# Values as the moving operand, heads divided and turned after the product, and a new order of all engines

## The reference

```python
qkv = x @ Wqkv                        # 128 -> 3 * 1024: 16 heads of 64
q = l2norm(q) * qs; k = l2norm(k) * ksc      # per head
# rotary turn of q and k
sim = einsum('bhwie,bhwje->bhwij', bq, bk2) * 8    # windows of 32 queries against 64 keys
attn = softmax(where(mask, -max, sim), -1)
out = einsum('bhwij,bhwje->bhwie', attn, bv2)
x = out.reshape(b, n, 1024) @ Wo + x
# feed-forward: layer norm, @ W1, a * gelu(gate), @ W2, + x
```

## Time and profile before

| | us |
|---|---|
| median of 3 runs | 3958.96 |
| lowest and highest | 3957.44 and 3965.38 |
| the profiled execution's own time | 3964.79 |
| its span (first to last instruction) | 3963.0 |
| PE busy | 3592.3 (91%) |
| DVE busy | 3253.2 (82%) |
| POOL busy | 2634.9 (66%) |
| ACT busy | 2372.4 (60%) |

### The profile page before, as it was taken

How to read it: one execution, slowest core, us unless ns; L and a number is a source line. 1 busy time by engine, 2 the same in 40 slices (tenths; PEclk the granted TensorE clock), 3 DMA queues, 4 the chain that set the end, 5 groups by cost and what they waited for, 6 DMA issues and landing times. The chain is left out here.

```text
span 3963.0 us, 156885 instructions
## 1 busy us (share of the span) xinstructions
PE 3592.3 (91%) x61680; PEld 2388.6 (60%) x61680; DVE 3253.2 (82%) x11525; ACT 2372.4 (60%) x4337; POOL 2634.9 (66%) x2556
## 2 busy tenths in 40 slices
PE   6799999999999999987699589999999999999997
PEld 4466666666666666652465356666666666666664
DVE  6888888888888888854899688888887888888884
ACT  2466667666666666663422156666666667666664
POOL 1787878877788778743000188787877788877872
PEclk9899999999999999997799689999999999999999
DMA  1232322322322322220000023233232232322222
GB/s 52 59 82 68 81 73 73 80 71 68 79 73 72 78 72 67 67 56 15 1 1 6 28 64 80 62 84 77 71 80 67 73 82 73 78 71 70 66 65 55
DMA packets 170283, 250.91 MB, mean 63 GB/s; under 512 B 36544, under 2 KB 67264, under 8 KB 169408
## 3 DMA queue, kind: packets, MB, share of 16 engines
q1 hardware_dynamic: 169536, 240.72, 24.4%
HBM read 38.21 MB, written 1.05 MB: 10 GB/s over the span
## 5 line engine op out<-in xcount | busy, mean ns | idle before, releaser
L1200 POOL TENSOR_TENSOR stack_roped<-stack_rot_c,stack_rot_s 128x512 f32<-128x512 f32 x768 | 966.3, 1273 | 420.9 <-DVE stack_rot_s L1020 420.9
L577 PE MATMUL stack_work<-stack_w_qkv,stack_xs 128*128 128x512 f32 x2304 | 1122.1, 603 | 36.3 <-ACT stack_sq L855 21.0
L1210 POOL TENSOR_TENSOR stack_roped<-stack_roped,stack_rnorm 128x512 f32<-128x512 f32 x768 | 784.6, 1043 | 175.9 <-DVE stack_rnorm L1052 175.9
L1018 DVE TENSOR_TENSOR stack_rot_c<-stack_work,rot_tables 128x512 f32<-128x512 f32 x768 | 518.3, 675 | 259.7 <-PE stack_work L577 256.5
L855 ACT ACTIVATE stack_sq<-stack_work 128x512 f32<-128x512 f32 x768 | 451.2, 598 | 367.7 <-DVE stack_rot_s L1020 367.6
L577 PEld LDWEIGHTS stack_work<-stack_w_qkv,stack_xs 128*128 128x128 f32 x2304 | 396.6, 193 | 335.1 <-issue 323.7
L626 PEld LDWEIGHTS stack_bank_o<-stack_p_t,stack_v_w 64*64 64x64 f32 x24576 | 405.4, 136 | 314.9 <-issue 308.8
L1063 DVE CUSTOM_DVE_ANT_0 stack_s_m<-stack_bank_s,band 128x64 f32<-128x64 f32 x3072 | 469.6, 218 | 137.4 <-PE stack_bank_s L600 126.0
L1029 DVE TENSOR_REDUCE stack_ssq<-stack_sq 128x8 f32<-128x512 f32 x768 | 519.8, 677 | 6.9 <-issue 6.6
L1020 DVE TENSOR_TENSOR stack_rot_s<-stack_work,rot_tables 128x512 f32<-128x512 f32 x768 | 522.0, 680 | 0.0
L1218 POOL TENSOR_TENSOR stack_s_m<-stack_s_m,stack_smax 128x512 f32<-128x512 f32 x384 | 421.2, 1097 | 114.9 <-DVE stack_smax L1063 113.5
(11 more groups left out here) (247 smaller groups left out, 5193.0 us busy)
## 6 DMA issues: line engine op xcount, KB each, us to landing
stack_v_w<-stack_v_nat SPq DMA_DIRECT2D x1152, 128.0 KB
stack_v_w<-stack_v_nat SPq DMA_DIRECT2D x768, 64.0 KB
stack_w_qkv<-table_ffn_qkv SPq DMA_DIRECT2D x192, 96.0 KB, 2.1
stack_w_o<-table_ffn_wo SPq DMA_DIRECT2D x12, 512.0 KB, 4.4
stack_w<-table_ffn_w SPq DMA_DIRECT2D x12, 384.0 KB, 3.2
stack_w<-table_ffn_w SPq DMA_DIRECT2D x12, 192.0 KB, 2.9
x_outer<-L_attn_a_X SPq DMA_DIRECT2D x4, 256.0 KB, 7.5
ret_xpos<-table_xpos SPq DMA_DIRECT2D x1, 1024.0 KB, 6.8
```

Source lines behind the costliest of these rows:

```text
L577: pe.matmul(bank[:, :], xs[:, T, :], w_qkv[:, g.half, col:col + 512], start=True, stop=True).then_inc(done["proj_" + c], 1)
L1018: dve.tensor_tensor(rot_c[:, i % 2, :].rearrange("p (h d) -> p h d", h=8), src.rearrange("p (h d) -> p h d", h=8), cosine, ALU.mult)
L1200: pool.tensor_tensor(roped[:, i, T % 2, :], rot_c[:, i % 2, :], rot_s[:, i % 2, :], ALU.add).then_inc(done["roped_" + c], 1)
L1210: pool.tensor_tensor(r, r, rnorm[:, T % 2, i, :].unsqueeze(2).broadcast_to([P, 8, HD]), ALU.mult).then_inc(done["united_" + c], 1)
```

## The change

1. The operands of `weigh` change places. The probabilities are now stationary (64x32) and the values move; each window's values have a 65th column of ones, so the product also gives the sum of the probabilities. The result is token by head.
2. `sum_probs`, `invert` and `scale_probs` go. `norm_heads` on DVE takes the reciprocal of the sums in `bank_o` and multiplies the heads by it, into `o_n`.
3. `turn_heads` on PE transposes `o_n`, four 128x128 transposes for each j, into a bank of `work`; `heads_out` copies from there.
4. Every engine has another order of steps, with other lags. On PE the two halves of `scores` and the two `weigh` steps are now apart, each with projections, transposes or `project_out` between it and the next. Before, `weigh` 1 and both halves of `scores` stood in a row.
5. ACT asks for its table once per group in place of twice, since the gelus stand elsewhere.

```diff
-        v_nat = sb("v_nat", [P, 2, 2, 8, HD])
-        v_w = sb("v_w", [P, 2, 4, 8, HD])
+        v_nat = sb("v_nat", [P, 2, 2, 8, HD + 1])
+        v_w = sb("v_w", [P, 2, 4, 8, HD + 1])
...
-                wait(pe, f"prob{j}", t)
+                wait(pe, f"exped{j}", t)
...
-                for half in range(2):
-                    for n in range(4):
-                        for odd in range(2):
-                            for gp in range(2):
-                                m, at = 2 * half + odd, P * half + WINDOW * n
-                                last = pe.matmul(bank_o[HD * odd:HD * (odd + 1), gp, at:at + WINDOW],
-                                                 v_w[64 * gp:64 * gp + 64, T % 2, n, 2 * m + j, :],
-                                                 p_t[64 * gp:64 * gp + 64, j, m, WINDOW * n:WINDOW * (n + 1)],
-                                                 start=True, stop=True)
+                for m in range(4):
+                    for gp in range(2):
+                        for n in range(4):
+                            last = pe.matmul(bank_o[WINDOW * n:WINDOW * (n + 1), gp, m * (HD + 1):(m + 1) * (HD + 1)],
+                                             p_t[64 * gp:64 * gp + 64, j, m, WINDOW * n:WINDOW * (n + 1)],
+                                             v_w[64 * gp:64 * gp + 64, T % 2, n, 2 * m + j, :], start=True, stop=True)
                 last.then_inc(done[f"weighed{j}"], 1)
+
+            def turn_heads(t, T, g, j, bank):
+                if not live(t):
+                    return
+                wait(pe, f"normed{j}", t)
+                for n in range(4):
+                    last = pe.transpose(bank[:, P * n:P * (n + 1)], o_n[:, j, n // 2, 2 * (n % 2):2 * (n % 2) + 2, :],
+                                        ident[:, :])
+                last.then_inc(done[f"pe_ot{j}"], 1)
...
-            def sum_probs(t, T, g, j):
+            def norm_heads(t, T, g, j):
                 if not live(t):
                     return
-                wait(dve, f"exped{j}", t)
-                wait(dve, f"inv{j}", t - 1)
-                dve.tensor_reduce(psum_p[:, j, :], s_m[:, T % 2, j, :, :], AX.X, ALU.add
-                                  ).then_inc(done[f"summed_p{j}"], 1)
-
-            def invert(t, T, g, j):
-                if not live(t):
-                    return
-                wait(dve, f"summed_p{j}", t)
-                wait(dve, f"prob{j}", t - 1)
-                dve.reciprocal(inv[:, j, :], psum_p[:, j, :]).then_inc(done[f"inv{j}"], 1)
+                wait(dve, f"weighed{j}", t)
+                heads = bank_o[:, :, 0:4 * (HD + 1)].rearrange("p f (h d) -> p f h d", d=HD + 1)
+                dve.reciprocal(inv[:, j, :, :].unsqueeze(3), heads[:, :, :, HD:HD + 1]).then_inc(done[f"inv{j}"], 1)
+                wait(dve, f"inv{j}", t)
+                wait(dve, f"pe_ot{j}", t - 1)
+                dve.tensor_tensor(o_n[:, j, :, :, :], heads[:, :, :, 0:HD],
+                                  inv[:, j, :, :].unsqueeze(3).broadcast_to([P, 2, 4, HD]), ALU.mult
+                                  ).then_inc(done[f"normed{j}"], 1)
```

More of the change, by code:

```diff
@@ L412, in ffn_stack @@
         BANK = {
[L413 to L417, removed]
+            "t_q0": (1, 0, 3, 1),
+            "t_k1": (2, 1, 1, 2),
+            "t_q1": (3, 2, 2, 3),
+            "ot0": (0, 1, 0, 0),
+            "ot1": (1, 2, 1, 1),
+            "p_q1": (0, 1, 2, 1),
+            "p_k1": (1, 3, 3, 0),
+            "wo": (1, 1, 2, 1),
+            "p_v0": (1, 3, 2, 3),
+            "p_q0": (3, 2, 3, 2),
+            "t_k0": (0, 3, 1, 0),
             "p_k0": (1, 0, 1, 0),
             "p_v1": (1, 3, 2, 3),
-            "wo": (0, 3, 1, 0),
-            "p_v0": (3, 1, 0, 1),
+            "pt0": (0, 3, 0, 3),
+            "pt1": (1, 0, 1, 0),
+            "wg1": 0,
+            "wg0": 1,
             "wg2": 0,
[L423 to L430, removed]
+            "wa0": 0,
+            "wa1": 2,
+            "wa2": 1,
+            "w2": 3,
+            "ct": 0,
             "va": 3,
-            "w2": 3,
-            "wg1": 0,
-            "wg0": 2,
         }
-        FIRST_IN, LAST_IN, LAST_UNIT, FIRST_PV, LAST_PV = "q0", "v0", "q1", 0, 1
+        FIRST_IN, LAST_IN, LAST_UNIT, FIRST_PV, LAST_PV = "q0", "v1", "q1", 0, 1
         def wait(eng, name, tile):
@@ L675, in slot @@
                 if T == 0:
[L676 to L685, removed]
@@ L686, in slot @@
-                    wait_group(pe, "hid1", G - 3)
[L687 to L703, removed]
@@ new lines, in slot @@
+                    wait(pe, "squared_k0", N - 2)
+                    turn(*at(4), "q0", work[(0 + row) % 4])
+                    scores(*at(5), 1)
+                    wait(pe, "v_out1", N - 5)
+                    turn(*at(4), "k1", work[(1 + row) % 4])
+                    wait(pe, "pt_set0", N - 6)
+                    turn(*at(4), "q1", work[(2 + row) % 4])
+                    wait(pe, "pt_set1", N - 6)
+                    turn_heads(*at(7), 0, work[(3 + row) % 4])
+                    wait(pe, "kept_q0", N - 4)
@@ new lines, in slot @@
+                    turn_heads(*at(7), 1, work[(0 + row) % 4])
+                    wait(pe, "kept_k1", N - 4)
+                    project(*at(2), "q1", work[(1 + row) % 4])
+                    wait(pe, "normed1", N - 7)
+                    weigh(*at(6), 0)
+                    wait(pe, "kept_q1", N - 4)
+                    project(*at(2), "k1", work[(2 + row) % 4])
+                    wait(pe, "ot_set0", N - 7)
+                    project_out(*at(7), work[(3 + row) % 4])
+                    wait(pe, "masked0", N - 5)
@@ new lines, in slot @@
+                    scores(*at(4), 0)
+                    wait(pe, "ot_set1", N - 7)
+                    project(*at(4), "v0", work[(0 + row) % 4])
+                    wait(pe, "squared_q1", N - 2)
+                    project(*at(1), "q0", work[(1 + row) % 4])
+                    wait(pe, "squared_k1", N - 2)
+                    turn(*at(3), "k0", work[(2 + row) % 4])
+                    wait(pe, "mid_set", N - 7)
+                    project(*at(1), "k0", work[(3 + row) % 4])
+                    wait(pe, "normed0", N - 6)
@@ L910, in heads_out @@
                     return
-                wait(act, f"weighed{j}", t)
+                wait(act, f"pe_ot{j}", t)
                 wait(act, "pe_wo", t - 2)
-                act.copy(o_t[:, T % 2, 4 * j:4 * j + 4, :].rearrange("p (g h) n -> p g h n", g=2),
-                         bank_o[:, :, 0:2 * P].rearrange("p g (h n) -> p g h n", h=2)
+                act.copy(o_t[:, T % 2, 4 * j:4 * j + 4, :],
+                         work[(BANK[f"ot{j}"][T] + g.row) % 4][:, :].rearrange("p (g n) -> p g n", g=4)
                          ).then_inc(done[f"ot_set{j}"], 1)
@@ L986, in slot @@
                 square(*at(0), "q1")
[L987 to L993 removed]
+                if T == 3:
+                    gelu(of(2), 1)
             act.wait_ge(consts_set, N_CONSTS * (run + 1))
```

388 lines of the change are left out of this document (192 added, 196 removed), and 2 rows, old and new, of the table NAMES.

## The result

The changed kernel takes 3929.23 us (median of 6 runs, 3927.77 to 3931.05), the kernel before in the same comparison 3961.39 us (6 runs, 3944.48 to 3971.79): a ratio of 0.9929, 95% interval 0.9905 to 0.9952. That is 0.7% faster, where 0.7% slower was forecast; 3929 also lies under the range. So the gain is small and was not found again in the later comparison; the forecast loss was found in neither.

What follows compares the result with a forecast made beforehand. It took PE to be bound by its own work and by pauses when instructions run out in dense runs. 3964.8 + 177 - 150 = 3992 us profiled, 3986 us as median; 3935 to 4090 at 8 in 10.

Steps and rivals of the forecast that it cites:

- 125 were forecast: PE's idle time: setting dense bursts apart gains 145.6 + 9 - 30 = 125 us, tiles outside the stretches included.
- 10 were left for them: PE's idle time under issue in scores and weigh would fall from some 120 us to near 10 us.
- rival C: PE's additional switches and the split overlap with other work and cost nothing, saving 108 us: 3878 us; chance 15%.
- rival B: PE's idle time does not depend on the bursts, so nothing is won: 4136 us; chance 10%.
- +177: Added PE work: 0.92 us per tile over 192 tiles, from values product, split scores, switches and turned heads.
- -150: Gain on PE from setting bursts apart: 125 us of idle time and 25 us of clock; bounds 0 and 185.
- 0.92 was forecast: Added PE time per tile: -0.52 values product, +0.13 split scores, +0.18 and +0.25 switches, +0.88 turned heads.
- 0.13 us: Scores in two halves on PE: 2 x 0.81 - 1.49 = +0.13 us per tile.
- the 67 us that the prediction's own sign named: Four slots without idle time take 67 us of PE; clearly less would be the sign of rival C.
- The clock, -25 us: PE's mean clock of 0.99 loses some 30 us over 2988 us; 25 of it counted as gained.
- Rival A: PE begins to wait for its banks, half a microsecond per tile or 96 us: 4082 us; chance 20%.
- the 20 us that the prediction named as its sign: PE's releasers naming ACT or DVE for more than 20 us would be the sign of Rival A.

Runs made afterwards that it cites:

- e4: The changed kernel with each of the four transposes of turn_heads done twice: 4077.4 us.
- e1: The kernel before with only PE's order changed, so that none of its four bursts of scores and weigh adjoin: 3915.8 us, ratio 0.9889 to the kernel before.
- e2: The kernel before with only weigh 1 moved away from the scores, which stay whole: 3861.2 us, ratio 0.9749 to the kernel before.
- e3: The changed kernel with weigh 1 and both halves of the scores in a row again: 4119.8 us, ratio 1.0399 to the kernel before.
- e6: e2 with weigh 0 also moved, from the slot's head to behind the turn of q1: 3844.7 us, ratio 0.9777 to the kernel before.
- e9: The changed kernel measured again, unaltered, in a later comparison: 3936.8 us, ratio 1.0006 to the kernel before.
- e11: The kernel of e5 measured again beside the changed kernel: 3875.5 us, ratio 0.9851 to the kernel before.
- e10: The changed kernel with the two halves of the scores in a row again, both weigh steps still apart: 3919.6 us, ratio 0.9960 to the kernel before.
- e5: e1 with the first half of the scores directly ahead of variance in slots with T = 1: 3872.4 us, ratio 0.9853 to the kernel before.
- e8: e2 with 64 transposes of the identity once ahead of the slots of each stack: 3859.3 us, ratio 0.9814 to the kernel before.

## Why the prediction was wrong

**What held.** PE sets the pace (e4). The idle time comes from dense runs (e1, e2, e3, e6) at the places where a packet of queue 8 is late, and setting them apart takes it away: 145.6 to 29.0 us in the stretches, and PE's idle time in the whole span falls from 370.7 to 243.5, 127 us where 125 were forecast. That it comes so near is in part luck: the pauses in `scores` and `weigh` fell to 6.0 us, where 10 were left for them, and new waits for `values_out`, which were put at nothing, took 18 us more than before. Each new switch has its price, in (0.09) and out (0.10), so rival C is wrong. The exchange of operands and the turned heads cost time: 8 x 0.11 - 2 x (1.07 - 0.79) = 0.32 us per tile, 61 us by that, and 61 us measured between e9 and e11, which differ in the engines' orders too. And "the idle time stays", rival B, is wrong. The rule of the Trainium skill beside it (Runtime: NRT & Kernel Launch, section "Instruction fetch mechanics") says that the supply is hidden except at branches; here it is not hidden in straight code, as the 77 pauses that end behind a packet show.

**What failed is the sum.** It is a small difference of two large terms, +177 and -150, and both were mis-sized, to the same side. In the profiled executions the change gave -35 us (3964.8 to 3929.6) in place of +27, 62 us apart.

1. *The added work, +177 us, is about +146.* This is the largest part, 31 us. The row for it is a group without pauses, before and after:

```profile
1137.36:1201.36 64.00, 63.96 (x1257) 43.49 (x1254) 57.77 (x222) 45.28 (x84) 52.03 (x52) 1.00 0.31 76
```

```profile
1126.78:1194.18 67.40, 67.01 (x1289) 44.29 (x1288) 59.47 (x223) 43.23 (x83) 45.67 (x45) 1.00 0.28 74
```

PE is busy for 3.05 us more per four tiles, 0.76 per tile; 0.92 was forecast. (By the length it is 3.4 us, but 0.35 of that is idle time, which belongs to the other term.) The bursts were read at 0.81 us and take 0.79, four times per tile: 0.08 of the 0.16. The rest lies in the kernel before. The prediction took 1.49 us for both halves of the scores in a row, from one place in the earlier trace rows. In the group above they take 1.51, 1.72, 1.51 and 1.63 us, 1.59 on average, so splitting them costs next to nothing (2 x 0.79 - 1.59) in place of 0.13 us. The 1.72:

```profile
1168.09 1.79 PE L600 MATMUL stack_bank_s<-stack_k_t,stack_q_t 64*32 64x64 f32 x128
1169.81 0.66 PE L585 MATMUL stack_work<-ident,stack_roped 128*128 128x128 f32 x4
```

The group after takes the 67 us that the prediction's own sign named; it is the group before that was taken too short.

2. *A pause is longer than its idle time, 22 us.* PE's idle time runs from the modelled end of a matmul to the next start. In the earlier trace rows the last pair before the pause starts at 2431.95 + 1.55 - 0.22 = 2433.28, and the next starts at 2435.44: 2.16 us from start to start, where 1.94 are called idle and 0.01 is the normal distance. There are 81 pauses in the scores and 30 in the values product, and each hides about 0.2 us, some 22 us in all by that estimate, in PE's busy time. The prediction counted the 145.6 as the whole.

3. *The clock, -25 us.* The prediction took 30 us of loss from a mean granted clock of 0.99, which is rounded and covers the stretches alone. Group 1335.64 to 1406.65 in the trace before lasts 71.01 us at a mean clock of 0.95; PE is busy for 67.48 us in it, 3.5 more than in the group at 1.00 above, a few tenths of it the hidden parts of its pauses. In the two stretches all groups of the trace after but the ones at a loop's turn have 1.00. Over the whole profiled execution the granted clock is 0.959 before and 0.968 after, which is 162 and 126 us short of the full clock: 37 us less, the most that the clock can have given back.

Added up: PE's idle time fell by 127 us and its busy time rose by 92. Of the busy time, +146 is the work and -22 the hidden part of the pauses, so some -32 are left for the clock, where 25 were counted. That makes the 62: 31 of work, 22 hidden, 7 of clock and 2 of idle time. How much of the 32 is the clock was not measured by itself. Only 16 of the 35 us lie in the two stretches (2987.7 to 2971.4); the other 19 lie for the most part in the filling and emptying of the stacks.

Rival A had a part of its mechanism right. The waits for `values_out`, 22.6 us, even cross the 20 us that the prediction named as its sign, and e1 and e10 show how quickly such waits come, but it is nothing near its 96. Two readings in the prediction are off without moving the forecast: at the head of a slot there are 28 transposes, not 32, and a group's 1254 pairs are 627 instructions per tile, not 642.

**The kernel before is not one number.** It took 3961, 3958, 3936 and 3934 us in four comparisons, and spread over 10 to 30 us within one; the changed kernel took 3929 and 3937 and spread over 3 to 9 us. The second and third comparison ran on the same chip, so the chip alone is not the cause. It may be that a kernel which lives with pauses depends on how fast each packet comes in that run, and one without them hardly does; that the packets' speed differs between the comparisons was not shown. So whether this change gains at all hangs on the comparison, while e2, e5 and e6 are faster in each comparison that held them.

## What to carry to other kernels

Read PE's idle time for "issue" in the middle of one straight group of small matmuls: if it is there, count the instructions in a row, and set such groups apart with long matmuls or transposes before changing what is computed. One move (e2) gave 2.5%, or 1.9% in its shifted form e8; splitting the scores as well (e5, 1.5% beside e8) gave part of that back, since each way in and out of small pieces costs 0.05 to 0.1 us and new waits came: break up only what outruns the supply. Look also at whether a packet of the instruction queue ends a fixed time ahead of each pause's end; this tells a late supply from other causes without a run. When a forecast is the difference of two terms over five times its size, the chance of a sign needs the error of both terms, and start-to-start times of a whole undisturbed group are a better basis than busy and idle sums.

## What the runs showed of the hardware

After 384 loads and matmuls in 2.3 us PE stood for up to 2.4 us (e3); after 256 in the scores alone the pauses were at most 1.2 us (e2); with 128 at a time and other work between they were nearly gone (4.7 us in e5's values product, none named in its scores). The pauses of over 1 us in the kernel before ended 1.19 to 1.56 us behind a packet of queue 8, all 77. The 64x32 form with 65 columns moved runs at the same pace as with 64, 0.79 us for 64 records from start to start, and the moved columns are not what limits them: the 64x64 form with 32 columns takes 1.07. DVE's multiplication out of the odd-strided bank took 692 ns, against 675 for the nearest row before.
